# A four-layer graph network on one core: one wide product in layer 3, and a prologue in another order with 198 scatters

## What is computed

```python
rhat = edge_attr / norm(edge_attr); sh1 = sqrt(3) * rhat
w0, w1, w2, w3, w4 = split(relu(edge_feature @ W_fc1) @ W_fc2, [64, 128, 160, 192])
xs, xv = s[dst], v[dst]
out0a = w0 * xs
out0b = w3 * einsum('emi,ei->em', xv, sh1) / sqrt(3)
out1a = (w1 * xs)[:, :, None] * sh1[:, None, :]
out1b = w2[:, :, None] * xv
out1c = w4[:, :, None] * cross(xv, sh1[:, None, :]) / sqrt(2)
agg = segment_sum(concat(out0a, out0b, out1a, out1b, out1c), src) / 32
```

## Time and profile before

| | us |
|---|---|
| median of 3 runs | 6171.2 (6168.77 to 6172.07) |
| profiled execution | 6174.38 |
| its span, first to last instruction | 6172.6 |
| mean granted TensorE clock | 0.944 of full |
| busy: TensorE / weight loads / VectorE / ScalarE / GpSimd | 4864.8 / 4236.5 / 4749.5 / 3638.6 / 4277.7 |

### The profile page before, as it was taken

One profiled execution on the slowest core, in us unless ns is written; L12 is line 12 of the kernel. 1 busy time (PEld: TensorE's weight loads), 2 busy tenths in 40 slices (PEclk: granted clock), 3 DMA queues, 4 the chain that ended last, 5 costly groups with the idle time before them and its releaser, 6 DMA issues.

```text
span 6172.6 us, 144969 instructions
## 1 busy us (share of the span) xinstructions
PE 4864.8 (79%) x37237; PEld 4236.5 (69%) x37237; DVE 4749.5 (77%) x14413; ACT 3638.6 (59%) x12787; POOL 4277.7 (69%) x4257
## 2 busy tenths in 40 slices
PE   0067778877784888888889799999999778888886
PEld 0037777777784777777777588777787657777775
DVE  8936777777774777777776399999999469999996
ACT  0026666666652666666665366666666457777774
POOL 1277777777767777777776677777777147777772
PEclk9999999999997999999999799999999879999998
DMA  3433333333333333333333333333333223333332
GB/s 114 156 70 73 75 75 75 75 76 75 75 72 74 74 75 75 75 75 75 74 75 76 97 79 79 78 79 79 79 79 71 61 72 83 82 83 82 81 78 59
DMA packets 599780, 487.85 MB, mean 79 GB/s; under 512 B 303546, under 2 KB 527161, under 8 KB 599421
## 3 DMA queue, kind: packets, MB, share of 16 engines
q0 software_dynamic: 189328, 317.19, 20.5%
q1 hardware_dynamic: 383286, 151.79, 10.3%
q10 hardware_dynamic: 27063, 17.73, 0.9%
HBM read 410.36 MB, written 75.56 MB: 79 GB/s over the span
## 4 chain that ended last, share of the span: by engine, by line
POOL 25%; issue 25%; DVE 21%; PE 14%; DMA 8%; DVEq 3%; ACT 1%; SPq 1%; POOLq 0%; ACTq 0%
POOL WK L654 12%; PE PS L879 8%; POOL TB L569 7%; POOL ACC L654 6%; DMA WK<-HT,WK 3%; PE PS L862 3%; DVE WK L1480 3%; DVEq L1448 2%; DMA WK<-PB 2%; DVE WK L1538 2%; DVE WK L1543 2%; DVE WK L1546 2%; DVE ACC L1131 1%; DVE ACC L1180 1%; DMA ACC<-HT,WK 1%
## 5 line engine op out<-in xcount | busy, mean ns | idle before, releaser
L1066 ACT ACTIVATE WK<-WK 128x64 f32<-128x64 f32 x9984 | 2471.2, 334 | 738.3 <-DVE WK L1493 373.8
L879 PE MATMUL PS<-WK 128*128 128x123 f32 (+1 forms) x21632 | 2730.0, 286 | 193.7 <-issue 193.7
L879 PEld LDWEIGHTS PS<-WK 128*128 128x128 f32 (+1 forms) x21632 | 2614.5, 199 | 354.5 <-issue 354.4
L654 POOL DMA_INDIRECT WK<-HT,WK x2080 | 2107.2, 1013 | 693.5 <-issue 618.7
L569 POOL DMA_INDIRECT TB<-WK x782 | 772.3, 988 | 354.6 <-issue 255.7
L654 POOL DMA_INDIRECT ACC<-HT,WK x832 | 797.9, 959 | 254.8 <-issue 243.1
L862 PE MATMUL PS<-F,WK 100*128 100x192 f32 x3360 | 662.0, 341 | 25.5 <-DVE WK L1511 24.4
L1047 ACT ACTIVATE WK<-PS 100x512 f32<-100x512 f32 x420 | 246.8, 588 | 690.2 <-PE PS L845 683.3
L867 PE MATMUL PS<-F,WK 64*128 64x224 f32 (+1 forms) x3360 | 417.4, 368 | 239.0 <-ACT WK L1050 213.1
L862 PEld LDWEIGHTS PS<-F,WK 100*128 100x128 f32 x3360 | 543.7, 192 | 84.9 <-DVE WK L1511 60.8
L654 POOL DMA_INDIRECT WOA<-HT,WK x416 | 500.6, 1203 | 128.8 <-issue 126.1
(11 more groups left out here) (229 smaller groups left out, 6537.1 us busy)
## 6 DMA issues: line engine op xcount, KB each, us to landing
WK<-TA SPq DMA_DIRECT2D x636, 72.0 KB
WK<-HT,WK POOLq DMA_INDIRECT x2080
WK<-TB SPq DMA_DIRECT2D x212, 144.0 KB
WK<-in_ea SPq DMA_DIRECT2D x23, 612.0 KB
TA<-WK POOLq DMA_DIRECT2D x23, 612.0 KB, 4.7
ACC<-HT,WK POOLq DMA_INDIRECT x832
WK<-in_eb SPq DMA_DIRECT2D x400, 32.0 KB
TB<-WK POOLq DMA_INDIRECT x782, 2.2
```

The source lines that it names most:

```text
L654: eng.indirect_dma_start(out=GB[l][u % 4][:, t, :], out_offset=None, in_=HT[:, :], in_offset=bass.IndirectOffsetOnAxis(ap=idx[:, t, vc:vc ...
L879: m = eng.matmul(psA[q][0:ch, k * BN:(k + 1) * BN], ms[:, t, k * ch:(k + 1) * ch], OH[q][:, t, :], start=(t == 0), stop=(t == G - 1))
L1066: m = eng.activation(m4[:, t, 96 + vb * c:160 + vb * c], TW[l][q][:, t, :], ACT.Copy, scale=tb[:, t, y1 + c:y1 + c + 1])
```

## The change

*Layer 2.* The products with w0 and w1 become one of 512 columns, written straight into the message rows (MA); ScalarE scales the part at 96 to 160 from there, in the order 1, 2, 0, the last in place. The wrap-around copy of tw goes to ScalarE, ahead of its scalings, and VectorE waits for it (`s_tw`) ahead of the cross product. The subtraction itself now increments the semaphore on which the others wait.

*Prologue.* SyncE's queue begins with keys, zero rows and the 23 loads of `in_ea`; the edge vectors, the weights and the nodes are loaded from ScalarE's queue, ahead of its square root. The flag is taken first. `keyB` goes first, with masks and scans in two halves of 391 columns, each half's part of PX is stored by ScalarE as soon as it is made, and SyncE and GpSimd go on to the scatters after the first half. `keyA` follows. 198 scatters stand in the prologue, 19 passes of layers 0 and 1 hold the others. ScalarE zeroes ACC, after the node phase. The small weight copies (`places`, 56) are issued in fives between chunks.

```diff
-SB0, SB1 = 102, 140
-NT0 = 25
+SB0, SB1 = 198, 140
+NT0 = 19
+HC = EC // 2
+PL0 = 8
...
+        MA = [m.rearrange("p (t f) -> p t f", t=G)[:, :, 0:192].rearrange("p t (a f) -> p t a f", a=2)[:, :, :, 0:64]
+              for m in MS[2]]
...
@ sync
-            eng.dma_start(X[:, :, :], A["x"].rearrange("(j p) d -> p j d", p=BN)).then_inc(s_x, 16)
...
-            eng.wait_ge(s_tb, 1)
-            eng.dma_start(PB.rearrange("(p c) f -> p (c f)", p=128), ACC[:, 0:EC * (RB - 64)]).then_inc(s_px, 16)
-            eng.wait_ge(s_px, 16)
+            eng.wait_ge(s_px[0], 16)
...
+            for x, (c, m) in enumerate(BCH[0]):
                 eng.wait_ge(s_free, k - 1)
                 rows_b(stage[k % 2], c, m, s_stg[k % 2])
                 k += 1
+                if x == PL0:
+                    eng.wait_ge(s_ws, 1)
+                    eng.wait_ge(s_wz, 5)
+                if x >= PL0:
+                    for d, o in places[(x - PL0) * 16:(x - PL0 + 1) * 16]:
+                        eng.dma_start(d, o).then_inc(s_wo, 16)
+            eng.wait_ge(s_px[1], 16)
...
@ gpsimd
-                if l == 0:
-                    eng.wait_ge(s_bk, NKEYS)
-                    eng.wait_ge(s_px, 16)
-                    eng.memset(ACC[:, 0:NB * p["nch"] * BN], 0.0).then_inc(s_az, 1)
...
@ scalar
+            eng.dma_start(sh, A["e3"].rearrange("(p c) f -> p c f", p=128)).then_inc(s_sh, 16)
+            eng.wait_ge(s_gm, 2)
+                for d, o in loads:
+                    eng.dma_start(d, o).then_inc(s_w, 16)
+            eng.dma_start(X[:, :, :], A["x"].rearrange("(j p) d -> p j d", p=BN)).then_inc(s_x, 16)
...
             eng.wait_ge(s_sq, 1)
             eng.activation(bq, bq, ACT.Sqrt, scale=1.0 / 3.0).then_inc(s_sqd, 1)
+            for x in range(2):
+                eng.wait_ge(s_tb, x + 1)
+                eng.dma_start(pv[:, x * HC:(x + 1) * HC, :], PX[:, x * HC:(x + 1) * HC, :]).then_inc(s_px[x], 16)
...
             phase(None, 0)
+            eng.wait_ge(s_px[0], 16)
+            eng.wait_ge(s_px[1], 16)
+            eng.wait_ge(s_wz, 5)
+            m = NB * LAYERS[0]["nch"] * BN
+            eng.activation(ACC[:, 0:m], ZERO[:, :].to_broadcast([128, m]), ACT.Copy).then_inc(s_az, 1)
...
+                    if l == 2:
+                        eng.wait_ge(e.D, i * (8 * ND[l]) + (u * ND[l] + KW))
+                        eng.activation(tw[:, :, 3:5, :], tw[:, :, 0:2, :], ACT.Copy).then_inc(s_tw, 1)
                     for t in range(G):
-                        for c in range(3):
-                            m = eng.activation(m4[:, t, 96 + vb * c:160 + vb * c], TW[l][q][:, t, :], ACT.Copy,
+                        for c in (1, 2, 0):
+                            m = eng.activation(m4[:, t, 96 + vb * c:160 + vb * c],
+                                               m4[:, t, 96:160] if l == 2 else TW[l][q][:, t, :], ACT.Copy,
...
@ vector, second key
+                    for x in range(2):
+                        cs = slice(x * HC, (x + 1) * HC)
+                        for q in range(NB):
+                            t = (cum, kf)[q % 2][:, 0:HC]
+                            v(eng.tensor_tensor_scan(t, half[x][:, q, 0:HC], z16[:, 0:HC], (OFF, OFH)[x][:, q:q + 1],
+                                                     ALU.add, ALU.add))
+                            w_()
+                            v(eng.copy_predicated(pos[:, cs], half[x][:, q, 0:HC].bitcast(U16), t))
+                        w_()
+                        if x == 0:
+                            eng.wait_ge(s_sqd, 1)
+                            v(eng.reciprocal(rec, bq))
...
@ vector, layer 2
-                            eng.wait_ge(e.N, i * 8 + (u + 3))
-                            kt = op(eng.tensor_tensor(TW[l][q], W[:, :, 64:128], e0, ALU.mult))
-                            assert kt == KT
+                            mt = op(eng.tensor_tensor(MA[q], W[:, :, 0:128].rearrange("p t (a f) -> p t a f", a=2),
+                                                      e0.unsqueeze(2).to_broadcast([128, G, 2, 64]), ALU.mult))
                             kw = op(eng.tensor_tensor(tw[:, :, 0:3, :], e1,
                                                       W[:, :, 192:224].unsqueeze(2).to_broadcast([128, G, 3, 32]), ALU.mult))
-                            op(eng.tensor_tensor(m4[:, :, 0:64], W[:, :, 0:64], e0, ALU.mult))
                             j = bucket(i, u)
                             need(kp)
                             kq = op(eng.tensor_tensor(tq[q], tp[q][:, :, 0, :], tp[q][:, :, 1, :], ALU.add))
-                            need(kw)
-                            kx = op(eng.tensor_copy(tw[:, :, 3:5, :], tw[:, :, 0:2, :]))
                             need(kq)
                             kr = op(eng.tensor_tensor(tq[q], tq[q], tp[q][:, :, 2, :], ALU.add))
-                            need(kx)
+                            op(eng.tensor_tensor(mv[:, :, :, 64:96], e1,
+                                                 W[:, :, 128:160].unsqueeze(2).to_broadcast([128, G, 3, 32]), ALU.mult))
+                            eng.wait_ge(s_tw, i * 8 + (u + 1))
...
-                            op(eng.tensor_tensor(mv[:, :, :, 96:128], mv[:, :, :, 96:128], tx, ALU.subtract))
-                            need(done)
-                            eng.sem_inc(e.M, 1)
+                            eng.tensor_tensor(mv[:, :, :, 96:128], mv[:, :, :, 96:128], tx, ALU.subtract).then_inc(e.M, 1)
```

More of the change, by code:

```diff
@@ L31 @@
 NCHA = EC // CHA
-SB0, SB1 = 102, 140
-NT0 = 25
+SB0, SB1 = 198, 140
+NT0 = 19
+HC = EC // 2
 SLOOP = NT0 * 8
-NMIN, NMAX = NT0 + 1, 31
+NMIN, NMAX = 26, 31
 assert SB0 + 2 * SLOOP + 2 * SB1 == EC and EC % CHA == 0
 BLK, LAG = 4, 10
+PL0 = 8
 NEV, SKB = 5, 8
@@ L166, in program @@
         masks = ACC[:, 0:NB * 391].bitcast(BF16).rearrange("p (b c) -> p b c", c=EC)
-        tb0 = NB * 391
+        half = [ACC[:, i * NB * 196:(i + 1) * NB * 196].bitcast(BF16).rearrange("p (b c) -> p b c", c=392) for i in range(2)]
+        spent = [ACC[:, 6272 + i * 391:6663 + i * 391].bitcast(BF16) for i in range(32)]
+        tb0 = NB * 392
         kf, bq, cum, pos = (ACC[:, tb0 + i * EC:tb0 + (i + 1) * EC] for i in range(4))
@@ L173, in program @@
         CF = NP[:, 410:411]
+        CH = [NP[:, 416 + i * NB:416 + (i + 1) * NB] for i in range(2)]
+        OFH = NP[:, 416 + 2 * NB:416 + 3 * NB]
         GI, CMP, BASF = NP[:, 640:896], NP[0:NB, 896:1152], NP[:, 1152:1408]
@@ L277, in program @@
         s_rt, s_rc = sem("s_rt"), sem("s_rc")
+        s_tw = sem("s_tw")
         class Edge:
@@ L693, in _ @@
             eng.wait_ge(s_gm, 4)
+            eng.wait_ge(s_cf, 1)
+            eng.matmul(psO[2][:, 0:1], ONE, CF, start=True, stop=True).then_inc(s_cg, 1)
             for b in range(NKEYS):
@@ L1115, in rank @@
                 eng.tensor_copy(ps, pos).then_inc(s_pos, 1)
-            for b, key in enumerate((keyA, keyB)):
+            v(eng.tensor_scalar(kf, keyA, 1.0, None, ALU.add))
+            w_()
+            eng.scalar_tensor_tensor(out=cum, in0=nxt, scalar=1.0, in1=kf, op0=ALU.add, op1=ALU.is_lt,
+                                     accum_out=CF).then_inc(s_cf, 1)
+            eng.wait_ge(s_cf, 1)
+            for o, (b, key) in enumerate(((1, keyB), (0, keyA))):
                 v(eng.tensor_scalar(kf, key, 1.0, None, ALU.add))
@@ L1119, in _ @@
                 w_()
[L1120 to L1124 removed]
+                v(eng.tensor_scalar(bq if b else cum, kf, float(-(BN + 1) // 2), 1.0 / BN, ALU.add, ALU.mult))
                 w_()
[L1126 removed]
+                v(eng.tensor_scalar(bq if b else cum, bq if b else cum, MAGIC, -MAGIC, ALU.add, ALU.add))
@@ L1173, in _ @@
                     with eng.If_ne(flag.val, 0):
+                        eng.wait_ge(s_px[0], 16)
+                        eng.wait_ge(s_px[1], 16)
+                        for q in range(NB):
+                            m = eng.tensor_scalar(masks[:, q, :], bb, float(q), None, ALU.is_equal, ALU.add,
+                                                  accum_out=CNT[:, q:q + 1])
+                        m.then_inc(s_mk, 1)
+                        eng.wait_ge(s_mk, 1)
                         rank(posA, 0, s_rk)
@@ L1177, in _ @@
                 else:
-                    for q in range(NB):
-                        t = (cum, kf)[q % 2]
-                        v(eng.tensor_tensor_scan(t, masks[:, q, :], z16, OFF[:, q:q + 1], ALU.add, ALU.add))
-                        w_()
-                        v(eng.copy_predicated(pos, masks[:, q, :].bitcast(U16), t))
-                    w_()
-                    v(eng.tensor_copy(PX[:, :, POSC - 64].bitcast(I32), pos))
-                    w_()
-            eng.wait_ge(s_sh, 16)
```

119 lines of the change are left out of this document (59 added, 60 removed).

## The result

The change saves 38 us where the forecast had 115: 6133.45 us median (6130.95 to 6135.0) against 6171.64, a ratio of 0.9939 (95% interval 0.9927 to 0.9952). The profiled execution has a span of 6133.2 us, 39.4 less than before. The measured time lies above the range.

A forecast was written before the change was run, and what follows sets the result against it. The prediction took GpSimd to bound layers 0 and 1's scatter units and VectorE layer 2, TensorE next. Its terms, -63 (layer 2), -44 (layers 0 and 1) and -8 (prologue), sum to -115: 6056 us, range 6005 to 6100.

The forecast's parts named there:

- TensorE's pair in layer 2: Layer 2: TensorE's work for two units can shrink to 11.41 us, 5.71 a unit.
- TensorE is what I expect to be late: Layer 2: once VectorE is relieved, TensorE sets the pace, taken as 5.72 us a unit instead of 6.02.
- the 5.45 of the sum: Layer 2: VectorE's own work per unit falls by 0.57 us to 5.45.
- +0.11 for the two sums: Layer 2, VectorE: L1529 and L1533 now stand side by side, the second waiting for the first's result, +0.11 us a unit.
- I read its 6.0 as following VectorE's beat: Layer 2 gathers: GpSimd's 6.0 us a unit only follows VectorE; floor 5.0, with 5.7 reachable with two holds of 0.34.
- rival 2: Layer 2: GpSimd keeps its 6.0 us by three holds per unit, giving 6119, or 6100 with part of the gain; chance 0.10.
- -44: Layers 0 and 1: 96 units that lose their scatter fall from 6.31 to 5.85 us each, -44 us.
- Rival 6: Layers 0 and 1: the edit fails, units stay at 6.2 us without scatters, 6089 in all; chance 0.07.
- -8: Prologue: layer 0's loop starts at 457 us instead of 465, -8 us.
- I keep 181, as a few us either way lie in the range: Prologue: first scatter kept at 181 us, though the node load might start the scatters up to 5 later.
- The paragraph on the node load: Prologue: node load on ScalarE's queue ahead of the square root, ending near 100 us undisturbed, near 160 if DMA engines are shared.
- the layer 2 term: Layer 2: 208 units at 5.72 instead of 6.02 us, -63 us.

The follow-up runs named there:

- e1: The changed kernel with 20 tiny VectorE instructions (one-column memsets) more ahead of layer 0: 6095.34 us, 0.9891 of the kernel before.
- e10: e1 with layer 2's wrap-around copy back on VectorE, behind the wide product: 6096.83 us, 0.9896 of the kernel before.
- e11: e1 with TensorE's order changed in layer 2, the even unit's bucket product ahead of its edge-weight product: 6036.56 us, 0.9795 of the kernel before.
- e2: The kernel before with 10 tiny VectorE instructions more ahead of layer 0: 6165.46 us, 1.001 of the kernel before.
- e18: e1 with e11's order and the node load behind the first chunk of scatters, 198 scatters in the prologue: 6018.73 us, 0.9767 of the kernel before.
- e16: e18 with the old division of the scatters, 102 in the prologue and 25 passes with one: 6044.83 us, 0.9807 of the kernel before.
- e4: e1 with the node load moved on ScalarE's queue behind the first store of the position table: 6088.58 us, 0.9884 of the kernel before.
- e7: The same kernel as e11, on a chip with TensorE's clock at 0.77: 0.9738 of the kernel before.
- e6: The same kernel as e10, on a chip with TensorE's clock at 0.77: 0.997 of the kernel before.

## Why the prediction was wrong, step by step

Two steps failed that carry 56 of the missing 76 us. VectorE's code ahead of layer 0 was priced by its own time alone and the loop behind it put at no cost, but the loop stood still 25 times for over 5 us (some 30 us). And TensorE's pair in layer 2 was put at 11.41 us and is 11.68 (26 us). The range ends at 6100. Without the first the change would have come to 6104 (an estimate by e1's ratio), without the second to 6107: each of them alone would have left it just above.

**Layer 2: mechanism right, a term mis-sized.** "TensorE is what I expect to be late" held: e10 and e11 show it, and VectorE's own unit (5.48) is close to the 5.45 of the sum. (The sum's +0.11 for the two sums is more than the 0.28 - 0.20 given for it, and yet what e11 shows: 0.31 instead of 0.20.) But the pair was put at 11.41 us and is 11.68. Two readings did that. The first L873 block was taken as 3.37 us from 4011.83 to 4015.20 in the earlier trace rows; that row has x31 where the others have x32. The view was asked from 4011.8 us on, and the block's first matmul lies ahead of that. The whole row is

```profile
4011.62 3.65 PE L879 MATMUL PS<-WK 128*120 128x123 f32 x32
```

and from its start to that of the next step are 3.58 us (3.57 after the change). So TensorE's work in a pair before was 11.9 of some 12.04 us, not 11.72. And L849 to L867 was to fall from 1.77 to 1.46 by an earlier start on ScalarE; it fell to 1.59: ScalarE now answers at once (L1062 from 4102.01 on, 0.69 after L843's start), and 0.51 us of waiting stay all the same. Together 0.33, less 0.06 for the L823 step (1.03 instead of 1.09): 0.27 a pair, 28 us in the layer, the 26 that were missing.

**Layer 2: the gathers.** "I read its 6.0 as following VectorE's beat" was right, and rival 2 wrong: GpSimd waits 2.00 us for TensorE in a pair. I had allowed two long gathers a unit; almost all are short now. Why so few, no run tested.

**Layers 0 and 1: the moved work gave most of its term, the sum did not hold.** -44 was 96 units by 0.46. Without the standstills the two layers are 17.9 and 12.9 us shorter in e1 than in e2 on the same chip, 31 in all; e18 against e16 gives 36. The units without a scatter are mostly slower than 5.85: the whole passes of them in e1 run at 5.94 to 5.97 us a unit in layer 0 and 5.84 to 6.50 in layer 1. The step that failed is one that the prediction doesn't have: that code in a loop which isn't touched costs the same as before. VectorE got 318 instructions more ahead of that loop (1240 instead of 922), and they were priced by their time alone. Rival 6 named the right place (the units of layers 0 and 1 without their gain), with the wrong reason and a chance of 0.07.

**Prologue.** -8 was forecast, +1.4 measured. The scatters' rate was right (266.7 us for 197 steps, forecast 273 for 198), the first scatter was 14 us late (195.35, forecast 181). "I keep 181, as a few us either way lie in the range" was the wrong choice. The paragraph on the node load had the cause, but looked only at the square root behind it, which came in time (142.77; ScalarE's queue was free at 140, between the 100 and the 160 of the forecast). What the load slowed was the other queue's table copy: 170 us instead of the 146 of the earlier trace rows, and 137 without the node load beside it (e4).

**What held.** ScalarE's copy was no burden, the wide product took 0.68, layer 3 kept its length and the stretches between the layers theirs within 5 us. The sign was right; of the 115 us the layer 2 term gave 37, and the other two edits, whose moved scatters alone are worth 26 us, were used up by layer 0's standstills and the late first scatter.

## What to carry to other kernels

When a change adds or removes instructions ahead of a loop with hundreds of instructions, look in the new profile for instruction packets in that loop and for "issue" idle of several us once per pass; some twenty harmless instructions cured it here and gave 0.5%. Before reading an engine's chain off a few rows, check that their counts are whole: a row at the edge of the window asked for is cut there. And where a transfer moves to another queue, ask whose packets it now runs beside, not only what stands behind it.

## What the runs showed that was not expected

- The same work at another place of VectorE's code: five instruction packets per pass, 5.3 to 6.3 us of standstill at the branch back to the loop's start, the granted clock down from 0.97 to 0.91, and 27 to 30 us for the layer, though VectorE was idle for 1.6 us in each unit of the kernel before.
- A copy of 0.29 us that costs its engine 0.08, since it stands between two steps of which the second waits for the first.
- The same kernel at 6160, 9603 and 10117 us on different chips; in the slow ones the granted clock was 0.77 and TensorE stood still in each pair besides. There the change of TensorE's order gave 2.3% (e7 against e6), on the others 1.0% (e11 against e10).
